# The chain to the next first attention inside a feed-forward stage: its parts reordered among the tiles, with context products first

## What is computed

```python
q = tanh(x @ W_charge.T + b_charge)[..., 0]
phi_c = mags * q[..., None] ** arange(ORDER + 1)            # 5 orders
shell = x @ W_shell.T + b_shell;  shell = shell / norm(shell)
proj = shell @ omega.T + rff_bias
phi_s = concatenate([cos(proj), sin(proj)], -1) * rff_scale
phi = (phi_c[..., :, None] * phi_s[..., None, :]).reshape(b, n, -1) @ W_combine.T
logits = where(causal, einsum('bnd,bmd->bnm', phi, phi) * T / temp, -inf)
out = einsum('bnm,bmd->bnd', softmax(logits), x @ W_v.T + b_v) @ W_out.T + b_out
```

## Time and profile before

| | |
|---|---|
| median of 3 runs | 3104.9 us (3096.24 to 3106.45) |
| the profiled execution | 3107.13 us, its span 3105.2 us |
| granted TensorE clock, mean | 0.857 of full speed |
| PE busy | 2298.2 us (74%) |
| DVE busy | 2176.1 us (70%) |
| ACT busy | 1065.5 us (34%) |
| POOL busy | 592.5 us (19%) |

### The profile page before, as it was taken

The page is one execution under the profiler, slowest core; times in us unless marked ns, Lnnn a source line. Parts: engine busy times, 40 slices in busy tenths (PEclk is TensorE's granted clock), DMA queues, the critical chain, the costliest instruction groups (busy, mean ns, idle before and its releaser), DMA issues.

```text
span 3105.2 us, 50667 instructions
## 1 busy us (share of the span) xinstructions
PE 2298.2 (74%) x17470; PEld 1851.3 (60%) x17470; DVE 2176.1 (70%) x4306; ACT 1065.5 (34%) x2004; POOL 592.5 (19%) x666
## 2 busy tenths in 40 slices
PE   3677788867666778886776787788667677788775
PEld 2556566656455656665655576666555566666663
DVE  5575788867746578886765657887675566788776
ACT  2322344422421244442242224444223223444314
POOL 2010322221011122221100212222110112222220
PEclk8688899988777889998877789999887788999988
DMA  6001589840000168983000108998100012899600
GB/s 227 0 1 53 118 158 164 155 92 1 1 15 10 44 139 157 172 155 64 1 1 15 53 17 162 163 168 139 37 1 1 14 53 56 160 169 170 117 1 14
DMA packets 658406, 251.37 MB, mean 81 GB/s; under 512 B 613082, under 2 KB 633946, under 8 KB 657370
## 3 DMA queue, kind: packets, MB, share of 16 engines
q1 hardware_dynamic: 653978, 243.79, 40.2%
q10 hardware_dynamic: 4160, 4.19, 0.4%
HBM read 52.87 MB, written 10.49 MB: 20 GB/s over the span
## 4 chain that ended last, share of the span: by engine, by line
PE 29%; issue 25%; DVE 22%; DMA 12%; ACT 6%; POOL 4%; DVEq 2%; SPq 1%; ACTq 0%; POOLq 0%
DMA l_ptb<-l_phb 6%; PE ps L233 6%; PE ps L235 5%; PE ps L234 5%; DMA l_pts<-l_phs 4%; DVE nmax L1361 3%; POOL d_pn L969 2%; DVE l_phb L1367 1%; DVE l_k L1416 1%; PE ps L1549 1%; DVE l_q L1420 1%; PE ps L1265 1%; DVE l_phs L1367 1%; ACT l_q L1327 1%; DVE xn L284 1%
## 5 line engine op out<-in xcount | busy, mean ns | idle before, releaser
L1361 DVE TENSOR_REDUCE nmax<-ps 128x1 f32<-128x1024 f32 (+7 forms) x512 | 383.0, 749 | 19.3 <-PE ps L1249 17.3
L1470 POOL CAST l_phb<-l_pb 128x1024 f16<-128x1024 f32 (+3 forms) x256 | 240.4, 939 | 668.9 <-ACT l_pb L1312 342.0
L1312 ACT ACTIVATE l_pb<-ps,nmax 128x1024 f32<-128x1024 f32 (+3 forms) x256 | 244.7, 956 | 275.3 <-DVE nmax L1361 274.6
L1247 PE MATMUL ps<-l_k,l_q 128*128 128x512 f32 (+3 forms) x768 | 317.0, 413 | 24.6 <-ACT l_ps L1312 24.2
L1367 DVE TENSOR_TENSOR l_phb<-l_pb,l_phb 128x1024 f16<-128x1024 f32 (+3 forms) x256 | 288.0, 1125 | 26.1 <-POOL l_phb L1470 24.2
L1248 PE MATMUL ps<-l_k,l_q 128*128 128x512 f32 (+3 forms) x768 | 269.3, 362 | 0.0
L1265 PE MATMUL ps<-l_v,l_ptb 128*128 128x64 f16 x4992 | 195.1, 196 | 50.7 <-DMA l_ptb<-l_phb 50.5
L1265 PEld LDWEIGHTS ps<-l_v,l_ptb 128*128 128x128 f16 x4992 | 174.5, 100 | 84.9 <-DMA l_ptb<-l_phb 56.3
L1470 POOL CAST l_phs<-l_ps 128x128 f16<-128x128 f32 (+3 forms) x256 | 129.4, 506 | 302.0 <-DMA l_pts<-l_phs 163.4
L233 PE MATMUL ps<-xTh,l_w 128*128 128x512 f32 x256 | 123.7, 483 | 85.2 <-DVE l_q L1420 50.4
L1247 PEld LDWEIGHTS ps<-l_k,l_q 128*128 128x128 f32 x768 | 155.0, 202 | 43.3 <-ACT l_ps L1312 29.9
(11 more groups left out here) (360 smaller groups left out, 6256.5 us busy)
## 6 DMA issues: line engine op xcount, KB each, us to landing
l_k<-xn SPq DMA_DIRECT2D x128, 256.0 KB, 4.0
l_w<-l_wqk_s SPq DMA_DIRECT2D x32, 512.0 KB, 4.9
l_wv<-l_wv_s SPq DMA_DIRECT2D x16, 512.0 KB, 6.5
xin<-in_x SPq DMA_DIRECT2D x4, 1024.0 KB, 5.4
m_w<-in_m_w SPq DMA_DIRECT2D x8, 512.0 KB, 4.3
m_w<-in_m_w SPq DMA_DIRECT2D x4, 1024.0 KB, 8.7
l_wo<-in_l_wo SPq DMA_DIRECT2D x16, 256.0 KB, 5.2
l_ptb<-l_phb SPq DMA_TRANSPOSE x256, 4.1
```

The costliest lines, as they stand in the source:

```text
L1247: pe.matmul(s[:, c0:c1], q, L["l_k1"][:, h, c0:c1], start=True, stop=False)
L1312: s.activation(l_numer(k)[:, 0:n], l_banks(k)[:, 0:n], ACT.Exp, bias=nmax[:, k % 4:k % 4 + 1], accum_out=lsum[:, h, k % NT:k % NT + 1]).th ...
L1361: v.tensor_reduce(nmax[:, k % 4:k % 4 + 1], l_banks(k)[:, 0:n], AX.X, ALU.max, negate=True).then_inc(q_["max"], 1)
L1470: g.tensor_copy(l_parts(k)[:, 0:cols], l_numer(k)[:, 0:cols]).then_inc(q_["hi"], 1)
```

## The change

- The context products (`x_pe_kv` and ACT's copies) leave part 5. They stand ahead of the feed-forward's first transposes, in banks 0 and 1, and ahead of the chain in the first element; C0's `m_bank` becomes 4.
- DVE's part 0, the norm, stands ahead of `hidden(0)`.
- Values 0 and 1 move from part 2 to part 5, values 2 and 3 from part 4 to part 7 (banks 2 and 3). The combine products take six banks, six in part 6 and two in part 7. The phi transposes move from part 8 to part 7.
- PE's part 7 stands behind `down(7)` and waits for its add. ACT's parts stand ahead of `silu(t+2)` and the copy of the transposed tile, with new numbers.
- DVE combines four token tiles in one instruction pair: a multiply and an add with `q` broadcast (`f_v_comb`), 18 instructions for all.
- `x_pe_u`, `x_a_u` and `x_v_u` move into the start of the attention.
- POOL adds the bias into `xin` in place, without waiting for the output transfer; the first `finish` waits for both, and reads `xin`.

```diff
             exp(0)
+            ahead()
             exp(1)
...
             maximum(1)
+            ahead()
             for k in range(n_bl):
...
@@ -508,9 +510,6 @@
             elif t == 2:
                 pe.wait_ge(s_lo, ln_done(b, 0))
                 for g in range(2):
-                    f_pe_value(pe, b, g)
-                for g in range(2):
-                    pe.wait_ge(a_sem["va"], b * 4 + g + 1)
...
             elif t == 4:
-                pe.wait_ge(a_sem["stl"], b * 2 + 2)
-                for g in range(2, 4):
-                    f_pe_value(pe, b, g)
                 for g in range(2):
-                    pe.wait_ge(a_sem["va"], b * 4 + g + 3)
+                    pe.wait_ge(a_sem["stl"], b * 2 + 2)
...
             elif t == 5:
-                pe.wait_ge(a_sem["u"], b * 2 + 2)
-                x_pe_kv(pe, C0, b)
+                for g in range(2):
+                    pe.wait_ge(a_sem["u"], b * 2 + g + 1)
+                    f_pe_value(pe, b, g)
             elif t == 6:
...
+                pe.wait_ge(C0.s["kvT"], b * 2 + 2)
+                for u in range(6):
                     if u % 4 == 0:
...
+                    if u >= 4:
+                        pe.wait_ge(a_sem["va"], b * 4 + u - 3)
+                    f_pe_comb(pe, u)
             elif t == 7:
...
+                for u in (6, 7):
+                    pe.wait_ge(a_sem["ya"], b * NT + u - 5)
+                    f_pe_comb(pe, u)
+                for g in (2, 3):
+                    pe.wait_ge(a_sem["ya"], b * NT + g + 1)
+                    f_pe_value(pe, b, g)
                 x_pe_m(pe, C0, b)
-            else:
-                pe.wait_ge(C0.s["ml"], b + 1)
-                pe.wait_ge(a_sem["phd"], b + 1)
                 for g in range(2):
+                    pe.wait_ge(a_sem["phd"], b * 2 + g + 1)
+                    pe.wait_ge(a_sem["ya"], b * NT + 5 + g)
...
                         last = pe.transpose(ps[:, 6 + g, u * P:(u + 1) * P], A["a_phi"][:, 4 * g + u, :], idf[:])
                     last.then_inc(a_sem["pt"], 1)
+            else:
                 pe.wait_ge(a_sem["qs"], b * 2 + 2)
...
-                x_pe_u(pe, C0, b)
...
+        def value_bank(g):
+            return 6 + g if g < 2 else g
+
+        def comb_bank(u):
+            return (0, 1, 2, 3, 6, 7, 0, 1)[u]
...
+                for g in range(2):
+                    f_a_value(s, b, g)
             elif t == 7:
+                for u in range(6):
+                    f_a_comb(s, b, u)
+            elif t == 8:
+                for u in (6, 7):
+                    f_a_comb(s, b, u)
+                for g in (2, 3):
+                    f_a_value(s, b, g)
                 x_a_m(s, C0, b)
-            else:
...
-                for m in range(ORDERS - 2, -1, -1):
...
+                f_v_comb(v, b, 0)
                 x_v_bias(v, C0, b)
             else:
+                f_v_comb(v, b, 1)
                 x_v_m(v, C0, b)
                 for g in range(2):
                     cols = slice(g * HALF, (g + 1) * HALF)
@@ -688,18 +692,32 @@
                     v.tensor_tensor(A["a_k2"][:, cols], ps[:, 6 + g, :], f32(A["a_k1"][:, cols]), ALU.subtract)
                 v.drain()
                 v.tensor_copy(A["a_qs"][64:128, :], f32(A["a_k2"][64:128, :])).then_inc(a_sem["qs"], 1)
-                x_v_u(v, C0, b)
+
+        def f_v_comb(v, b, g):
+
+            four = slice(4 * g, 4 * g + 4)
+            q = A["a_q"][:, four].unsqueeze(2).to_broadcast([P, 4, COMB])
+            acc = A["a_acc"][:, four, :]
+            v.wait_ge(a_sem["ya"], b * NT + 4 * g + 4)
+            for m in range(ORDERS - 2, -1, -1):
+                src = A["a_y"][:, four, (m + 1) * COMB:(m + 2) * COMB] if m == ORDERS - 2 else acc
+                v.tensor_tensor(acc, src, q, ALU.mult)
+                v.drain()
+                v.tensor_tensor(acc if m else A["a_phi"][:, four, 0:COMB], acc, A["a_y"][:, four, m * COMB:(m + 1) * COMB], ALU.add)
+                v.drain()
+            v.tensor_copy(A["a_phi"][:, four, COMB:2 * COMB], A["a_phi"][:, four, 0:COMB]).then_inc(a_sem["phd"], 1)
...
         def f_g(g, b):
 
+            x_diagonal_first(g, b)
+            g.wait_ge(s_xn, b * (NPH * NT) + NT)
+            g.tensor_tensor(xin[:], xin[:], bvo[:].unsqueeze(1).to_broadcast([P, NT, D]), ALU.add).then_inc(s_xb, 1)
...
+        def x_diagonal_first(g, b):
             g.wait_ge(C0.s["kvT"], b * 2 + 2)
             x_diagonal(g, C0, b)
-            g.wait_ge(s_out, b * 16 + 16)
-            g.wait_ge(s_xn, b * (NPH * NT) + NT)
-            g.tensor_tensor(x[:], xin[:], bvo[:].unsqueeze(1).to_broadcast([P, NT, D]), ALU.add).then_inc(s_xb, 1)
...
         def a_v(v, b):
-            v.wait_ge(s_xb, b * 4 + 1)
...
             def finish(k, h, i, o, r):
-                v.scalar_tensor_tensor(out=x[:, i, :], in0=o, scalar=r, in1=x[:, i, :], op0=ALU.mult, op1=ALU.add).then_inc(s_xu, 1)
+                if k == 0:
+                    v.wait_ge(s_xb, b * 4 + 1)
+                    v.wait_ge(s_out, b * 16 + 16)
+                v.scalar_tensor_tensor(out=x[:, i, :], in0=o, scalar=r, in1=xin[:, i, :], op0=ALU.mult, op1=ALU.add).then_inc(s_xu, 1)
...
-        C0 = Cross("x0", 1, XH0, XD0, 6, 6, 6)
+        C0 = Cross("x0", 1, XH0, XD0, 0, 4, 6)
...
+            if more:
+                pe.wait_ge(C1.s["sm"], b * NT + NT)
+                x_pe_kv(pe, C0, b + 1)
             turn_x(0)
             pe.wait_ge(g_sem["xT"], b * 2 + 1)
+            if more:
+                pe.wait_ge(C0.s["kvT"], (b + 1) * 2 + 2)
             updown(0)
...
-                if more:
+                if more and t < NT - 1:
+                    if t == 6:
+                        pe.wait_ge(g_sem["gh"], b * NT + NT)
                     f_pe(pe, b + 1, t)
                 down(t)
+                if more and t == NT - 1:
+                    pe.wait_ge(s_xu, b * (NPH * NT) + NPH * NT)
+                    f_pe(pe, b + 1, t)
             if more:
                 f_pe(pe, b + 1, NT)
-                pe.wait_ge(s_xu, b * (NPH * NT) + NPH * NT)
...
+            if more:
+                f_v(v, b + 1, 0)
             hidden(0)
...
-                if more:
+                if more and t >= 1:
                     f_v(v, b + 1, t)
...
+            if more:
+                x_a_kv(s, C0, b + 1)
             copy_x(0)
...
                 s.activation(G["g_r"][:, t % 2, :], G["g_h"][:, t % 2, :], ACT.Copy, bias=MAGIC, scale=G["g_hs"][:, t:t + 1]).then_inc(g_sem["gr"], 1)
+                if more:
+                    f_a(s, b + 1, t)
                 if t + 2 < NT:
...
                 s.copy(G["g_hT"][:, t % 2, :], psb(4)).then_inc(g_sem["hT"], 1)
-                if more:
-                    f_a(s, b + 1, t)
...
-            att_a(s, AT0, bl0, b, lambda k: A["a_sm"][:, k % 2, :])
+            att_a(s, AT0, bl0, b, lambda k: A["a_sm"][:, k % 2, :], lambda: x_a_u(s, C0, b))
...
+                if t == 6:
+                    s.wait_ge(s_ws, 64)
+                    x_a_kv(s, C0, 0)
                 f_a(s, 0, t)
...
+            x_pe_kv(pe, C0, 0)
```

More of the change, by code:

```diff
@@ L419, in att_pe, with att_a @@
                 hook("end", k)
-        def att_a(s, at, bl, base, src, hooks={}):
+        def att_a(s, at, bl, base, src, ahead, hooks={}):
             n_bl = len(bl)
@@ L587, in f_a @@
                 s.activation(A["a_q"][:], A["a_sh"][:, :, 64], ACT.Tanh).then_inc(a_sem["q"], 1)
-            elif t == 4:
-                for g in range(2, 4):
-                    f_a_value(s, b, g)
-            elif t == 5:
+            elif t == 6:
                 for g in range(2):
```

54 lines of the change are left out of this document (18 added, 36 removed).

## The result

The changed kernel took 3016.0 us (median of 4 runs, 3010.53 to 3026.1), the kernel before 3102.8 us on the same chip (median of 4, 3096.24 to 3106.45). The ratio is 0.973, with a 95% interval of 0.970 to 0.976: 87 us faster, where 70.5 were forecast. The profiled executions have spans of 3105.2 and 3016.0 us.

What follows compares the result with a forecast made beforehand. No engine is full; the transitions from g_xq to the first score bound it, the first taking 124.05 us. Savings of 17.5 + 17.1 + 20.0, plus 15.9 in the first chain, take 70.5 from 3104.9: 3034, range about 3005 to 3055.

Steps and rivals of the forecast that it cites:

- rival B: PE stays at the higher clock level through the end of the chain: 6.5 us per transition, 3015; chance 0.27.
- the stall: POOL's add in place holds up DVE beside hidden row 0, 1.8 us per transition, and at the first chain's angles, 4.1.
- Up to the combine products: From g_xq to PE's combine products, moved norm, values and context products build a lead of about 15 us.
- The end of the chain: From the combine products to the query/key rows: ready at 875.8 instead of 887.96, lead 12.2, or 10.4 after POOL's add.
- the clock level: PE at the lower level from the combine products on: six token tiles 5.2 us, down product 1.9, values 5.1.
- ACT's parts: ACT's parts ahead of silu and the transpose copy: inputs there in time, or silu and copy still in time; cost 0.
- Rival D: ACT's parts ahead of silu and transpose copy make hidden row and down product wait: slower, 3124; chance 0.05.
- Behind a_qs: From query/key rows to first score, 14.34 us become 2.3 before the score plus 3.7 for PE's jump (bounds 0.9 and 4.1).
- The attention's head: x_pe_u, x_a_u and x_v_u between the attention's first and second softmax cost 1.2 us, four times (bounds 0 and 2.5).
- The signs: Expected in the trace: g_xq to first score 106.6, 106.8 and 102.9 us, or about 100 under rival B.
- The first chain: The chain before the first element: 29.1 us removed, 12.0 added, net 17.1, less 1.2 for the attention's head: 15.9.
- The sum: Whole kernel: three transitions and the first chain, 17.5 + 17.1 + 20.0 + 15.9 = 70.5 us saved.

Runs made afterwards that it cites:

- e11: The changed kernel with DVE's norm of the next element back in tile 0, behind the first hidden rows: 3035.9 us.
- e1: The changed kernel with the context products and ACT's two copies back in part 5, behind the angles and ahead of values 0 and 1: 3068.9 us.
- e12: The changed kernel with POOL's add waiting for the first half of the projection, meant to run beside DVE's angles: 3028.0 us.
- e6: The changed kernel with POOL's add waiting for both halves of a_qs, so that it runs beside the first score: 3008.2 us.
- e10: The changed kernel with ACT's parts back behind the copy of the transposed tile, not ahead of silu and that copy: 3040.4 us.
- e3: The changed kernel with POOL again waiting for the output transfer and writing x, and DVE waiting for it before the first score: 3030.4 us.
- e2: The changed kernel with x_pe_u, x_a_u and x_v_u back at the chain's end and gone from the attention: 3034.8 us.
- e5: The changed kernel with the loop over the elements written out on PE, DVE, ACT and POOL: 3001.2 us.
- e7: The changed kernel with PE's wait for the last add moved from ahead of the last two combine products to ahead of x_pe_m: 3005.2 us.
- e8: The changed kernel with each half of DVE's combination made tile by tile again, 16 scalar_tensor_tensor and a copy: 3027.5 us, ratio 0.973 to the kernel before.
- e4: The changed kernel with value products 0 and 1 back in part 2, and 2 and 3 in part 4, all in banks 6 and 7: 3043.9 us.

## Why the prediction was right, and where it was off

The range held the time, and the direction and the places of the gain were right; the time is rival B's 3015 rather than the forecast's 3034. That it is B's to 1 us is luck: B gives the higher level 6.5 us per transition and leaves the stall in, and the runs show at most 3.9 for the level and no stall there. Step by step, as lead over the kernel before in the first transition:

| at | forecast | measured |
|---|---|---|
| PE's first products of tile 2 | 1.1 | 2.0 (33.53 to 31.57 behind g_xq) |
| DVE's shell part | 3.9 | 5.2 (46.14 to 40.91) |
| angles | 6.2 | 7.6 (65.29 to 57.74) |
| combine products | 15 | 15.5 (86.43 to 70.94) |
| a_qs | 10.4 | 16.4 (109.02 to 92.62) |
| first score | 18.7 | 23.9 |

**Up to the combine products** the walk held, with the norm undersized: 2.0 there, and e11 loses 3.2 without it. (e11's 34.57 at that place is 1.0 later than the 33.53 of the kernel before, so something else in the change costs 1.0 there, which no edit isolates.) The context products were the largest term as forecast; their price of 10 stood in e1 as 10.4.

**The end of the chain** is the step that failed, by 6 us per transition. Two terms were wrong. First, the clock level. The forecast took the lower level from the combine products on; the rows show the higher one for six combine products and the down product (3.2 us) and the lower one only for the last two and the values behind them. From the first combine product to the last write of a_qs the forecast had 26.3 us, and it took 22.4. Rival B was right for the first half and the forecast for the second. Secondly, the stall of 1.8 us: POOL's add stands at 768.65 beside hidden row 0, and no DVE instruction there is longer than usual; the 128x1 scalar step took 0.15 us. The remaining 0.3 us were won before the combine products.

```profile
771.15 0.15 DVE L1646 TENSOR_SCALAR g_hm<-g_hm 128x1 f32<-128x1 f32 x1
```

My reason, that it reads and writes SBUF, was too coarse: e12 shows that of such steps a wide one is held and this one isn't. The first rounding, at 774.84, escapes the add's end (773.17) by 1.7 us.
The Trainium skill ("SBUF — State Buffer", Who interferes with whom) has 2-port modes and two SBUF inputs block against GpSimd. For the wide tensor_scalar e6 and e12 agree (4.55 and 3.02 us instead of 0.42 and 0.68); the short one and the reduction ran free.

**ACT's parts** were put at 0, and e10 makes their place worth 6 us per transition, 2.5 up to the combine products and most of the rest by the level. So this term had no sound reason: without ACT's order the lead at the combine products is 13.0, and the forecast's 15 came out because its walk over the waits of DVE and PE took ACT's results to be there in time, which e10 shows they aren't without the new order. Rival D, which saw only harm in this order, is refuted. The lesson is in the method: I had asked of each part whether its input is there when ACT reaches it, and not who waits for its output.

**Behind a_qs** the 14.34 us became 2.2 + 4.6 in the first transition against 2.3 + 3.7, and the jump is 4.8 in the second: both are above the upper bound of 4.1. The third transition has no jump, as said. That the tail was "the output transfer's and POOL's" was true of the kernel before, but e3 shows that POOL's add in place is worth only 0.4 to 0.7 us where PE jumps, and 4.5 where it doesn't; by e3's rows what frees the rest of the tail is that x_pe_u and x_a_u no longer stand ahead of the transfer's issue. No run puts both back together.
The Trainium skill ("Runtime: NRT & Kernel Launch", Instruction fetch mechanics) makes a taken branch whose target is outside the fetched window wait for a fetch. The rows agree on three engines as to the wait: 4.6 us on PE, 4.0 on DVE, 3.6 on ACT, and none of it when the loop is written out. The fetch itself is in no row.

**The attention's head** was put at 4.8 in all and costs 0.2 from the kernel before to the changed one (194.18 to 194.35 over four), 1.1 by e2: the small waits of DVE and ACT do hide it.

**The signs.** The 106.6 us from g_xq to the first score that the forecast gave hold this head's 1.2, which lies behind the first score. By its own terms they were 105.4, and B's about 99; measured are 100.1.

**The first chain** was forecast at 17.1 before the head's cost. Measured from PE's first transposes it is 20.3 (78.93 to 58.60). POOL's stall came at the size given, 4.1, but for another reason: the angles' step that is held, L670, has one SBUF operand and not two. The rest is again the level: eight combine products took 3.78 us instead of the 6.94 of the earlier trace rows. But e5, e7, e8, e10 and e12, in which PE has the same instructions up to there, took 6.77 for them and 61.9 to 62.3 for the chain, a gain of 16.7 to 17.0, the forecast's 17.1.

**The sum.** 93.7 us won in the stages against 70.5 forecast: 18 in the three chains up to a_qs, 4.8 for the head, 2.2 in the first chain (its norm began 1.0 later, so 20.3 count as 19.3), less 1.8 for what stands behind a_qs. Then 4.5 lost elsewhere, the head's 0.2 among them, which no edit here explains.

## What to carry to other kernels

When work is threaded into another stage's loop, ask of each piece who waits for its output, not only whether its input is there: the same ACT instructions one or two places earlier were worth 6 us per transition, half of it with the clock. Look for waits that stand ahead of work which does not need them; moving one wait down behind the last two combine products and the values (e7) brought a_qs 5.5 us earlier per transition, half of it by the clock, and the first score 4.7 where PE jumps. The last instruction of a loop body pays for the jump: work that depends on nothing can lie under it, but on each engine separately.

## What the runs showed of the hardware that I had not expected

- **The same PE instructions at the same distances ran at different levels.** First chain, changed kernel first, then e7:

```profile
100.00:110.00 10.00, 9.69 (x74) 9.37 (x75) 6.03 (x15) 7.01 (x16) 0.00 (x0) 0.99 0.00 1
```

```profile
100.00:110.00 10.00, 10.00 (x39) 9.45 (x39) 3.79 (x9) 6.15 (x13) 0.00 (x0) 0.50 0.00 0
```

  In one the level rose at about 101 us, in the other it stayed low to 110: some 3.5 us of difference in a stretch whose PE instructions no edit touches. In e10 PE was busy for 6.35 of 8 us and stayed at 1.2 GHz. What decides the moment of the rise is left open. Inside the transitions most kernels had the same pattern in all three, with small shifts: the changed kernel's last two combine products took 1.96, 1.37 and 1.97 us.
- **A taken loop jump costs 4.6 us on PE, 4.0 on DVE and 3.6 on ACT**, each engine on its own (e5, e2). On PE it is 4.6 to 5.4 in the kernels that have nothing under it, the most in e4 and e7.
- **A wide DVE tensor_scalar from SBUF to SBUF waits until a POOL tensor_tensor beside it ends** (4.55 instead of 0.42 us, 3.02 instead of 0.68), while a reduction over 1024 columns, a scalar_tensor_tensor with one PSUM operand and a 128x1 tensor_scalar run on (e12), as does a tensor_tensor with one PSUM operand (e6, 1.23 us).
